# A new table of units for GpSimd's indirect transfers of rows to the experts

## The reference, cut to what matters

```
x = x + 0.5 * L0_ffn(layernorm(x))            # 8 experts, top 2 of 8
x = x + L0_attn(layernorm(x))                 # 16 heads, keys halved by a convolution
x = x + 0.5 * L0_ffn(layernorm(x))            # 8 experts
x = x + 0.5 * L1_ffn(x)                       # causal attention, then 16 experts (top 2, capacity 512)
x = x + L1_attn(x)                            # causal attention
x = x + 0.5 * L1_ffn(x)                       # causal attention, then 16 experts
```

## Time and profile before

| what | value |
|---|---|
| time, median of 3 runs | 1873.56 us (1871.69 to 1874.87) |
| span of the profiled execution | 1910.5 us; no time of its own is given beside the span |
| TensorE busy | 1556.0 us, 81% of the span |
| VectorE busy | 1307.4 us, 68% |
| GpSimd busy | 1077.0 us, 56% |
| ScalarE busy | 968.9 us, 51% |
| mean granted TensorE clock | 0.887 of full |

### The profile page before, as it was taken

The page is one execution under the profiler, slowest core; times in us unless marked ns, Lnnn a source line. Parts: engine busy times, 40 slices in busy tenths (PEclk is TensorE's granted clock), DMA queues, the critical chain, the costliest instruction groups (busy, mean ns, idle before and its releaser), DMA issues. The chain is left out here.

```text
span 1910.5 us, 46442 instructions
## 1 busy us (share of the span) xinstructions
PE 1556.0 (81%) x17682; PEld 947.9 (50%) x17682; DVE 1307.4 (68%) x3414; ACT 968.9 (51%) x2039; POOL 1077.0 (56%) x1712
## 2 busy tenths in 40 slices
PE   5548888885599998885899499999999999866992
PEld 5432333344355554543677255555555555435772
DVE  7348897883588887766321588888888787775224
ACT  4124667652256676552233166777777766531331
POOL 3436767514467857654354376465566767552552
PEclk9966999987689999886799599999999999975996
DMA  8442323212533222210353343233232223102445
GB/s 279 128 127 86 109 70 95 78 30 83 146 99 115 91 82 78 88 36 22 99 152 102 117 128 105 79 94 103 79 114 82 83 92 103 47 26 62 148 123 160
DMA packets 233187, 188.24 MB, mean 99 GB/s; under 512 B 30035, under 2 KB 221306, under 8 KB 232326
## 3 DMA queue, kind: packets, MB, share of 16 engines
q1 hardware_dynamic: 222582, 166.36, 29.1%
q0 software_dynamic: 10240, 18.89, 3.1%
q10 hardware_dynamic: 144, 0.00, 0.0%
HBM read 104.34 MB, written 80.74 MB: 97 GB/s over the span
## 5 line engine op out<-in xcount | busy, mean ns | idle before, releaser
L1015 DVE TENSOR_REDUCE mx<-PS 128x2 f32<-128x512 f32 (+3 forms) x1408 | 784.3, 612 | 193.2 <-PE PS L653 138.2
L865 ACT ACTIVATE pt<-PS 128x512 f32<-128x512 f32 (+2 forms) x1408 | 669.6, 537 | 311.5 <-PE PS L653 227.9
L670 PE MATMUL PS<-ka,qa 52*128 52x256 bf16 (+3 forms) x2048 | 467.0, 307 | 67.1 <-DVE mx L1015 49.3
L786 PE MATMUL PS<-qa,ka 55*128 55x512 bf16 (+3 forms) x1792 | 462.2, 322 | 33.6 <-DMA qa<-nm 26.5
L730 PE MATMUL PS<-pt,vs 128*32 128x512 f32 (+3 forms) x3584 | 353.1, 484 | 3.7 <-issue 3.0
L653 PE MATMUL PS<-mask_q,identh 64*128 64x64 bf16 x3072 | 301.3, 193 | 0.7 <-issue 0.7
L653 PE MATMUL PS<-mask_k,identh 64*128 64x64 bf16 x3072 | 299.6, 192 | 0.5 <-issue 0.5
L786 PEld LDWEIGHTS PS<-qa,ka 55*128 55x128 bf16 x1792 | 167.6, 94 | 262.6 <-issue 102.7
L653 PEld LDWEIGHTS PS<-mask_k,identh 64*128 64x128 bf16 x3072 | 250.2, 97 | 51.1 <-issue 6.6
L653 PEld LDWEIGHTS PS<-mask_q,identh 64*128 64x128 bf16 x3072 | 254.3, 98 | 30.2 <-issue 8.2
L670 PEld LDWEIGHTS PS<-ka,qa 52*128 52x128 bf16 x2048 | 172.8, 95 | 98.1 <-DVE mx L1015 61.2
(11 more groups left out here) (249 smaller groups left out, 2353.2 us busy)
## 6 DMA issues: line engine op xcount, KB each, us to landing
pt<-in_f_w SPq DMA_DIRECT2D x96, 256.0 KB
qa<-q_parts SPq DMA_DIRECT2D x256, 96.0 KB
ka<-k_parts SPq DMA_DIRECT2D x192, 96.0 KB
q_parts<-parts SPq DMA_DIRECT2D x32, 384.0 KB, 3.0
k_parts<-parts SPq DMA_DIRECT2D x24, 384.0 KB, 2.6
xn<-y_rows SPq DMA_DIRECT2D x32, 256.0 KB, 3.2
hid<-y_rows SPq DMA_DIRECT2D x32, 256.0 KB, 3.5
q_parts<-parts SPq DMA_DIRECT2D x32, 256.0 KB, 3.1
```

Source lines behind the costliest of these rows:

```text
L670: mm = pe.matmul(PS[:, bank, i * n:(i + 1) * n], k.qa[rows, b % 2, g, h // 2, qb * P:(qb + 1) * P], k.ka[rows, b % 2, g, h // 2, 0:n], sta ...
L786: mm = pe.matmul(PS[:, bank, i * n:(i + 1) * n], k.ka[rows, b % 2, g, h // 2, kb * P:(kb + 1) * P], k.qa[rows, b % 2, g, h // 2, q0:S], st ...
L865: nc.scalar.activation(k.pt[:, u % 2, at[c]:at[c] + len(heads) * n], PS[:, SC_BANK + c % RING, 0:len(heads) * n], ACT.Exp, scale=SCORE_SCA ...
L1015: nc.vector.tensor_reduce(out, PS[:, MX_BANK + t % RING, 0:len(heads) * n] .rearrange("p (h n) -> p h n", n=n), AX.X, ALU.max).then_inc(s. ...
```

## The change

Only the table and the loop that reads it are changed: a unit may now have pieces of two phases. All 64 transfers of each pass are still issued, in the same order among themselves, with the same waits.

```
-    SENT_IN = {t - 13: (0, t, t + 1) for t in range(8)}
-    SENT_IN |= {-5: (1, 8, 11), -4: (1, 11, 14), -3: (1, 14, 16), -2: (2, 16, 20), -1: (3, 20, 24)}
+    SENT_IN = {-11: ((0, 0, 2),), -10: ((0, 2, 3),), -8: ((0, 3, 5),), -7: ((0, 5, 8),), -5: ((1, 8, 11),), -4: ((1, 11, 12),),
+               -3: ((1, 12, 14),), -2: ((1, 14, 16), (2, 16, 18)), -1: ((2, 18, 20), (3, 20, 24))}
...
                 if r.sent and u - U in SENT_IN:
-                    phase, first, end = SENT_IN[u - U]
-                    send(pool, k, r, phase, range(first, end))
+                    for phase, first, end in SENT_IN[u - U]:
+                        send(pool, k, r, phase, range(first, end))
```

## The result

| what | before | after |
|---|---|---|
| median of 8 runs each | 1873.8 us (1871.69 to 1877.75) | 1866.34 us (1862.79 to 1869.96) |
| ratio to before, 95% interval | | 0.995 (0.9937 to 0.9964) |
| span of the profiled execution | 1910.5 us | 1865.4 us |

The changed kernel is 7.5 us faster by the medians, 9.4 us by the ratio (6.7 to 11.8). The forecast was 1862.5 in a range of 1857.5 to 1869.5; by the median alone the first rival's 1867.5 lies nearer.

What follows compares the result with a forecast made beforehand. TensorE waits for the maxima `nm`, late behind GpSimd's transfers. 11.1 + 1.1 - 0.4 - 0.3 = 11.5 us off the 1910.5 us span, scaled to 11.3, gives 1862.3, stated as 1862.5; range 1857.5 to 1869.5.

Steps and rivals of the forecast that it cites:

- the first rival: Waits for `nm`: only the waits come back, and less of them without profiler, about 6 us, 1867.5; chance 0.18.
- Units U-13, U-12 and U-9: They lose their two transfers; waits for `nm` go and the whole excess of 6.07 and 5.08 us returns.
- The spot checks of the prediction: Last 13 units: waits for `nm` under 0.3 us, casts within 0.3 us of copy, five units 45 to 46 us.
- Units U-11, U-8 and U-7: They get four, four and six transfers, mostly hidden; 0.4 us charged, between 0 and 3.
- Unit U-4: Goes from six transfers to two, so a 1.10 us wait goes; 1.1 us gained, between 0 and 2.2.
- The tail: Two more tiles behind each pass's last split, hidden before the experts' first load; 0.3 us charged, between 0 and 2.8.
- The rival of the tail: Behind attention 3's loop, ten of 36 transfers taking 3.04 us make the kernel slower, about 1881; chance 0.05.
- The loss of 8.3 us: Four transfers beside VectorE's marking of rows could each take the long form; the gain would be about 6.

Runs made afterwards that it cites:

- `before_again`: The kernel before, profiled once more with no edit: 1873.57 us, ratio 0.9991.
- the first half: The new table for tiles 0 to 8: 7.7 us off with it alone, 11.6 us from the changed kernel against a table with only the rest new.
- `tail18`: A table with 16 tiles behind the last split (1857.51 us), with tiles 14 and 15 moved from U-3 to U-2, making 18: 1863.48 us, ratio 0.9940.
- `tail20`: Two tiles more than `tail18` behind the last split, 20 in all: 1878.21 us, ratio 1.0013.
- `early_half`: The new table for tiles 0 to 8, the table of the kernel before for the rest: 1868.30 us, ratio 0.9959.

## Why the prediction was right, and where it was not

The forecast of 11.3 us stands against 9.4 by the ratio (6.7 to 11.8) and 7.5 by the medians. The mechanism and the sign were right. That the size fits is in part luck: two terms were too small by about the same, with opposite signs.

*Units U-13, U-12 and U-9: right.* The whole excess comes back, not the waits alone. It is larger in an ordinary execution: 51.59 - 45.20 and 51.34 - 45.20, 12.5 us against 11.1 charged. The waits of `before_again` there sum to 0.91 + 2.36 + 0.91 and 0.90 + 2.36 + 0.93, 8.4 us; the first rival took these for all that comes back, and the table refutes it in the traces. In the runs the two readings of the first half, 7.7 and 11.6 us, average 9.7: nearer the forecast's 11.1 than the rival's 6, but each of these two lies outside one of the intervals. The spot checks of the prediction hold in these units: no wait for `nm`, the casts behind the splits of U-13 and U-9 0.1 us after the copy, 45 to 46 us. Over all 13 units they do not: the 1.50 us at U-3 of attention 3 is above the 0.3 that I had named (it was 1.09 in `before_again`).

*Units U-11, U-8 and U-7: right.* Nothing was lost there. After the first tile of a pack GpSimd waits 1.07 to 2.02 us for a landing in attention 2, which made U-7's six transfers end only at 783.6, and TensorE still does not wait for `nm` there. 0.4 was charged, 0 measured.

*Unit U-4: mis-sized.* "I take the middle, 1.1 us" between 0 and 2.2. The waits at the start of U-2 were 4.40 and 2.99 us in `before_again` and are absent after. The interval from the copy in U-3 to that in U-2 falls from 15.84 to 11.24 and from 14.41 to 11.42, 7.6 us. The bound from above came from one wait of 1.10 us in attention 2, and the profile on record has 1.07 in attention 3. In it the cast behind the six transfers starts 5.0 and 5.3 us after ScalarE's copy has ended, in `before_again` 8.4 and 6.8. Of the 3.3 us more in attention 2, 2.1 are a longer wait for a landing between the first two of the three tiles (2.88 instead of 0.74); the rest, like the 1.5 us in attention 3, is that the copy comes sooner after the six have begun.

*The tail: the step that failed.* "3.4 to 4.4 us are free, so the delay is hidden" and "In attention 2 the wait is 10.52 us against 7 us of new work: hidden". Neither cover was there. The waits that were to take up the new work are 5.60 and 3.89 us in `before_again`, so the last phase starts 6.15 and 4.85 us after the `slot` instead of 0.78: 5.4 and 4.1 us late where I had 0 and 1.7 to 2.8. And I took the transfers to be out of the way 2.6 us after the last one begins, when its rows land. In all eight traces since, the load goes out 5.72 to 5.74 us after the last one ends, whatever VectorE does, because GpSimd's drain at the end of the block ends only 5.28 to 5.29 us after it. The trace on record has that row too (attention 3), and I had not read it:

```profile
L639 POOLq DRAIN  x1: 11984/11984/11984, 1737.8 to 1737.8; - x1
```

This drain ends at 1749.75, 5.28 us after 1744.47, and VectorE's at 1750.13, so some 0.4 us were free and not 3.4; the load goes out 1750.56 - 1744.47 = 6.09 us after the last transfer. The cost is 66.39 - 62.96 and 65.93 - 62.26, 7.1 us, where I charged 0.3. It is less than 5.4 + 4.1 because the last `slot` comes 1.75 and 0.25 us sooner behind the copy and the last phase itself is 0.2 us shorter in each pass. By my own test, "if the experts' first load waits for the last transfer", this part of the prediction was wrong: the first load comes behind GpSimd, and `tail18` and `tail20` show by two doses that each transfer counts.

*The sum.* 12.5 + 7.6 - 7.1 = 13.0 from the terms; other intervals of the next five units give 1.4 back (1.1 of it from U-6 to U-5 in attention 3), so the traces have 11.7 us and the runs 9.4. The stretches that no table touches differ more than that between executions: from the first copy to the last of attention 1 it is 250.00 to 254.03 us, and all of them together take 1529.1 us in `before_again` and 1533.0 to 1540.9 in the seven changed tables. So one trace of each kernel can't tell 11.7 from 9.4. For `early_half` the stretches have 13.7 and the runs 7.7 (4.9 to 10.5); its other stretches take 1540.9 us, 11.8 more than those of `before_again`, and whether that is chance or a price of the table one trace can't say. It stays open.

*The rival of the tail.* It was the right place with the wrong cause: I let it decide only if some ten transfers took the long form. The one long transfer of the record began at 1723.20, 0.3 us into four instructions of VectorE's marking of rows, and ended 0.85 us after the last of them:

```profile
1722.90 2.49 DVE L463 TENSOR_TENSOR pt<-row_names,places 128x1024 bf16<-128x1024 bf16 x4
```

All twelve transfers above 1.6 us in the nine traces began within such a run of VectorE and ended 0.84 to 0.85 us after it; two more that began there took only 1.28 and 1.29 us. The Trainium skill (SBUF — State Buffer, Who interferes with whom) says that a transfer issued by GpSimd is starved while VectorE holds the port pair that they share. The traces agree with that in these twelve, though no experiment has moved VectorE's work to test it, so the long row of the record did not speak against the rule, as I had it. The loss of 8.3 us that I had worked out for the rule did not come: the longest of the changed kernel's 128 transfers took 1.672 us, the median 0.972, and at the end they take 0.97 each. Length was not needed; number was enough. The loss was there and was outweighed.

## What to carry to other kernels

Work is hidden only up to the moment that the next stage can start, and that moment has to be measured for each engine: from the last instruction of each to the first of the next stage, in more than one execution, since the engine with the constant distance is the one that binds. The instruction with which each engine leaves the block belongs to that look: here GpSimd's stood in the first trace. A move that frees a wait in the middle and lengthens a stage's end should be split into its two halves; the better version here kept the first and paid for the room with one tile in an emptier unit. And a slack or a wait read once, in a long execution, is no bound: read a second profile of the same kernel before sizing terms with it.

## What the runs showed of the hardware

- GpSimd's drain at the end of a block ends 5.28 to 5.29 us after the end of its last indirect transfer, in all eighteen ends of attentions 2 and 3 in nine traces; without such transfers, at the end of attention 1, it takes 0.52 us. Where it ends last, in sixteen of them, the next block's first instruction of VectorE comes 5.6 us after that transfer and SyncE's load 5.73. From VectorE's last instruction it can be as little as 0.69 us. The landing does not set it: the last transfer lands 1.15 to 1.79 us after its end, and the drain does not move with that. What the drain does in the rest no row shows.
- The granted clock is 1.00 of full, the 2.4 GHz level, over the 45.20 us in which TensorE never waited for `nm`, and 0.93 and 0.97 over the same instructions with three waits of up to 2.36 us in each. The waits of 8.4 us cost 12.5 there; the lower clock behind them is one part of the difference.
- In a pack of tiles GpSimd waits for a landing between two tiles of the same phase, 0.70 to 2.60 us in the changed kernel and some 0.75 in most cases, so a tile of a pack can take up to 1.9 us longer than usual: in attention 2 U-8's second tile starts 2.02 us after the first has ended.
- The twelve of GpSimd's 1152 indirect transfers in nine traces that took more than 1.6 us (1.67 to 3.04, where the median is 0.97) all began while VectorE ran its 128x1024 bf16 instructions of line 463 back to back, and ended 0.84 to 0.85 us after the last of them. Not every transfer that begins there is held so long: two took 1.28 and 1.29 us.
